# The two Mamba scans of a four-block kernel: from a scan by state over 128 channels to scan tiles of 32 channels x 4 states

## What is computed

```
xz = x @ Win.T ; u, z = split(xz)                        # 256 channels each
u  = silu(causal_conv4(u) + convb)
dtr, B, C = split(u @ Wx.T, [8, 24])                      # 16 states
dt = softplus(dtr @ Wdt.T + bdt) ; A = -exp(Alog)         # [256, 16]
h[t] = exp(dt[t] * A) * h[t-1] + (dt[t] * u[t]) * B[t]    # 256 x 16 states
y[t] = sum over n of h[t, :, n] * C[t, n] + u[t] * D
out  = (y * silu(z)) @ Wout.T
```

## Time and profile before

| | us |
|---|---|
| median of 3 runs (1869.71 to 1870.5) | 1870.18 |
| the profiled execution | 1869.97 |
| its span in the trace | 1868.0 |
| forward pass: preparation / scan / output | 82.55 / 241.65 / 13.4 |
| backward pass: preparation / scan | 76.85 / 242.05 |

### The profile page before, as it was taken

The page is one execution under the profiler, slowest core; times in us unless marked ns, Lnnn a source line. Parts: engine busy times, 40 slices in busy tenths (PEclk is TensorE's granted clock), DMA queues, the critical chain, the costliest instruction groups (busy, mean ns, idle before and its releaser), DMA issues. The chain is left out here.

```text
span 1868.0 us, 19573 instructions
## 1 busy us (share of the span) xinstructions
PE 1461.9 (78%) x6816; PEld 551.5 (30%) x6816; DVE 1388.6 (74%) x1944; ACT 948.8 (51%) x1147; POOL 375.1 (20%) x349
## 2 busy tenths in 40 slices
PE   0441499999999999999665777766577777699998
PEld 0220022222222222222221222232122223467776
DVE  8933899999999999994467999964799997311111
ACT  2220077777777777778445555523555453244332
POOL 1201000000000000000203666640266665000000
PEclk9765599999999999999876999997599999699999
DMA  0021010001000000000000000000000000000000
GB/s 28 0 76 70 25 53 1 1 31 44 2 1 38 38 2 1 2 1 1 11 0 0 1 0 1 1 5 6 0 1 1 0 1 3 22 14 23 11 23 22
DMA packets 19444, 26.14 MB, mean 14 GB/s; under 512 B 4078, under 2 KB 13958, under 8 KB 19358
## 3 DMA queue, kind: packets, MB, share of 16 engines
q1 hardware_dynamic: 19358, 25.06, 3.9%
HBM read 20.56 MB, written 4.19 MB: 13 GB/s over the span
## 5 line engine op out<-in xcount | busy, mean ns | idle before, releaser
L655 DVE TENSOR_REDUCE at_mpart<-psum 128x1 f32<-128x512 f32 x1024 | 656.8, 686 | 49.5 <-PE psum L720 39.7
L634 ACT ACTIVATE at_probs<-psum 128x1024 f32<-128x1024 f32 x512 | 496.2, 1021 | 273.3 <-PE psum L745 273.1
L1070 ACT ACTIVATE psum<-m_dt,m_aneg 128x512 f32<-128x512 f32 x256 | 176.9, 692 | 224.2 <-DVE m_h L1098 224.2
L716 PE MATMUL psum<-at_ks,at_qs 64*128 64x512 bf16 x512 | 207.7, 406 | 86.1 <-DMA at_km<-k_parts 51.8
L758 PE MATMUL psum<-at_probs,at_vg 128*32 128x512 f32 x2048 | 273.6, 606 | 0.4 <-ACT at_probs L634 0.4
L745 PE MATMUL psum<-at_qs,at_ks 75*128 75x512 bf16 x1024 | 269.1, 384 | 1.3 <-ACT at_probs L634 0.2
L720 PE MATMUL psum<-at_km,at_qm 64*128 64x512 bf16 x512 | 207.7, 406 | 0.0
L1112 POOL TENSOR_TENSOR msb_hc<-m_h,msb_crow 128x512 f32<-128x512 f32 x128 | 159.7, 1269 | 155.8 <-DVE m_h L1098 155.8
L1112 POOL TENSOR_TENSOR msf_hc<-m_h,msf_crow 128x512 f32<-128x512 f32 x128 | 159.7, 1269 | 145.0 <-DVE m_h L1098 143.8
L1141 PE MATMUL psum<-msb_hc,ident 128*128 128x512 f32 x256 | 142.9, 644 | 55.0 <-POOL msb_hc L1112 48.9
L1141 PE MATMUL psum<-msf_hc,ident 128*128 128x512 f32 x256 | 142.2, 640 | 55.5 <-POOL msf_hc L1112 49.2
(11 more groups left out here) (245 smaller groups left out, 1344.9 us busy)
## 6 DMA issues: line engine op xcount, KB each, us to landing
at_qs<-q_parts SPq DMA_DIRECT2D x48, 96.0 KB
at_ks<-k_parts SPq DMA_DIRECT2D x48, 96.0 KB
xe_w<-in_w SPq DMA_DIRECT2D x16, 256.0 KB
q_parts<-ap_parts SPq DMA_DIRECT2D x1, 1536.0 KB, 5.3
k_parts<-ap_parts SPq DMA_DIRECT2D x1, 1536.0 KB, 5.3
at_qm<-q_parts SPq DMA_DIRECT2D x16, 96.0 KB
at_km<-k_parts SPq DMA_DIRECT2D x16, 96.0 KB
l_x<-in_x SPq DMA_DIRECT2D x4, 256.0 KB
```

The lines of the kernel that those rows point to most:

```text
L634: act.activation(probs[:, u % 2, p, :], s_pair[p], ACT.Exp, scale=float(HD) ** -0.5).then_inc(probs_ready, 1)
L655: dve.reduce_max(mpart[:, s % 2, 2 * jp + b, i, kc:kc + 1], ring[x % 3], AX.X).then_inc(ring_free, 1)
L716: pe.matmul(ring[x % 3], S.qs[0:HALF, buf, q], S.ks[0:HALF, buf, k], start=True, stop=True)\
L1070: act.activation(decay[b], S.dt[:, b, cols(k)], ACT.Exp, scale=S.aneg[:, NS * b + n:NS * b + n + 1]).then_inc(decay_ready, 1)
```

## The change

**Preparation.** The convolution moves into the weights: VectorE multiplies the u half of Win by the four taps, PE adds four products over shifted inputs in PSUM, and ACT applies silu with the bias straight from PSUM, by chunks of 512, through a ring of 8 PSUM banks. B and C are no longer split; B, C, dt and dt*u are stored to DRAM by chunks. GpSimd makes dt*u.

**Scan.** A scan tile has 32 channels x 4 states on its 128 partitions. `k` runs over 4 chunks x 2 blocks x 4 groups of states x 4 groups of channels, 128 steps; 16 steps are a block. dt and dt*u of a block (copied to the four groups of partitions) and B and C of a chunk (spread over 32 partitions each) come from DRAM by DMAs of 32 partitions. In a step GpSimd makes dt*u*B, ACT the decay, VectorE scans into PSUM and then weighs the tile of the step before by C. ACT keeps the last column. Every four steps PE adds four tiles by four products of 32 output columns each.

The diff, cut to its core:

```diff
@@ -872,10 +870,18 @@
...
 BC = 2 * NS
...
+GC = 32
+SP4 = P // GC
+NQ = NS // SP4
+NJ = P // GC
+NTILE = (DI // GC) * NQ
...
 def mamba_prep_stage(nc, S, dr, d):
...
@@ -886,154 +892,163 @@
...
+        soft, dt, dtu = sb("soft", [P, NB, T]), sb("dt", [P, NB, T]), sb("dtu", [P, NB, T])
...
+        UZ = 2 * NB * NCH
+        ORDER = [("x", 0)]
+        for c in range(NCH):
+            if c + 1 < NCH:
+                ORDER.append(("x", c + 1))
+            ORDER += [("d", c, b) for b in range(NB)]
+        USE = {key: UZ + n for n, key in enumerate(ORDER)}
...
         @block.sync
...
+            for k in range(KC):
+                sp.dma_start(taps[:, k, :], dr["taps"][d, k:k + 1, :].to_broadcast([P, DI])).then_inc(taps_in, 16)
...
+            for c in range(NCH):
+                sp.wait_ge(ring_free, USE["x", c] + 1)
+                sp.dma_start(S.bc_dram[:, cols(c)], bcx[0:BC, cols(c)]).then_inc(bc_stored, 16)
+            for c in range(NCH):
+                sp.wait_ge(dt_ready, c + 1)
+                sp.dma_start(S.dt_dram.rearrange("(b p) t -> p b t", p=P)[:, :, cols(c)],
+                             dt[:, :, cols(c)]).then_inc(dt_stored, 16)
+                sp.wait_ge(dtu_ready, c + 1)
+                sp.dma_start(S.dtu_dram.rearrange("(b p) t -> p b t", p=P)[:, :, cols(c)],
+                             dtu[:, :, cols(c)]).then_inc(dtu_stored, 16)
...
         @block.gpsimd
...
+            for c in range(NCH):
+                pool.wait_ge(dt_ready, c + 1)
+                pool.tensor_tensor(dtu[:, :, cols(c)], dt[:, :, cols(c)], S.u[:, :, cols(c)],
+                                   ALU.mult).then_inc(dtu_ready, 1)
...
         @block.scalar
...
+            for c in range(NCH):
+                for b in range(NB):
+                    act.wait_ge(ring_full, use + 1)
+                    act.activation(S.u[:, b, cols(c)], ring[use % R], ACT.Silu, bias=V(f"{name}_convb{b}"))\
+                        .then_inc(ring_free, 1)
+                    use += 1
+                for b in range(NB):
+                    act.wait_ge(ring_full, use + 1)
+                    act.activation(S.zs[:, b, cols(c)], ring[use % R], ACT.Silu).then_inc(ring_free, 1)
+                    use += 1
...
+            for key in ORDER:
+                act.wait_ge(ring_full, use + 1)
+                if key[0] == "x":
+                    act.activation(bcx[:, cols(key[1])], ring[use % R][0:BC + DR, :], ACT.Copy).then_inc(ring_free, 1)
+                else:
...
+                    act.activation(soft[:, b, cols(c)], ring[use % R], ACT.Abs, bias=V(f"{name}_bdt{b}"))
+                    act.activation(dt[:, b, cols(c)], ring[use % R], ACT.Relu, bias=V(f"{name}_bdt{b}"))\
+                        .then_inc(ring_free, 1)
+                    if b == NB - 1:
+                        act.wait_ge(ring_free, use + 1)
+                        act.activation(soft[:, :, cols(c)], soft[:, :, cols(c)], ACT.Exp, scale=-1.0).then_inc(exp_ready, 1)
+                use += 1
+            for c in range(NCH):
+                act.wait_ge(exp_ready, c + 1)
+                act.activation(soft[:, :, cols(c)], soft[:, :, cols(c)], ACT.Ln, bias=1.0).then_inc(ln_ready, 1)
...
         @block.vector
...
+            for c in range(NCH):
+                dve.tensor_scalar(xm[:, KC - 1 + c * CH:KC - 1 + (c + 1) * CH], S.xh[:, d, cols(c)], V("norm_g"), V("norm_b"),
+                                  ALU.mult, ALU.add).then_inc(xm_ready, 1)
+                if c == 0:
+                    dve.wait_ge(taps_in, 16 * KC)
...
+                    dve.tensor_tensor(taps[:, :, :], taps[:, :, :],
+                                      w_in_sb[:, 0:DI].unsqueeze(1).to_broadcast([P, KC, DI]), ALU.mult).then_inc(taps_ready, 1)
             for b in range(NB):
...
+            for s in range(SP4):
...
+            for c in range(NCH):
+                dve.wait_ge(ring_free, USE["d", c, NB - 1] + 1)
+                dve.wait_ge(ln_ready, c + 1)
+                dve.tensor_tensor(dt[:, :, cols(c)], dt[:, :, cols(c)], soft[:, :, cols(c)], ALU.add).then_inc(dt_ready, 1)
...
         @block.tensor
...
+            pe.wait_ge(taps_ready, 1)
...
+            for c in range(NCH):
+                pe.wait_ge(xm_ready, c + 1)
                 for b in range(NB):
...
+                    for k in range(KC):
+                        mm = pe.matmul(ring[use % R], taps[:, k, P * b:P * (b + 1)], xm[:, c * CH + k:(c + 1) * CH + k],
+                                       start=(k == 0), stop=(k == KC - 1))
+                    mm.then_inc(ring_full, 1)
+                    use += 1
                 for b in range(NB):
...
+                    pe.matmul(ring[use % R], w_in_sb[:, DI + P * b:DI + P * (b + 1)],
+                              xm[:, KC - 1 + c * CH:KC - 1 + (c + 1) * CH], start=True, stop=True).then_inc(ring_full, 1)
+                    use += 1
+            for key in ORDER:
...
+                if key[0] == "x":
+                    c = key[1]
+                    pe.wait_ge(ring_free, 2 * NB * c + NB)
+                    for b in range(NB):
+                        mm = pe.matmul(ring[use % R][0:BC + DR, :], w_x[:, b, :], S.u[:, b, cols(c)],
+                                       start=(b == 0), stop=(b == NB - 1))
+                else:
...
+                    pe.wait_ge(ring_free, USE["x", c] + 1)
+                    mm = pe.matmul(ring[use % R], w_dt[BC:BC + DR, P * b:P * (b + 1)], bcx[BC:BC + DR, cols(c)],
+                                   start=True, stop=True)
+                mm.then_inc(ring_full, 1)
+                use += 1
...
 def mamba_scan_stage(nc, S, dr, d):
...
@@ -1047,98 +1062,146 @@
...
+        PB = NQ * NJ
+        PC = NB * PB
+        NK = NCH * PC
+        ND, NI, NH2 = 3, 4, 3
...
+        def at(k):
+            c, rest = divmod(k, PC)
+            b, rest = divmod(rest, PB)
...
+        dts, dus = sb("dts", [P, 2, NJ, CH]), sb("dus", [P, 2, NJ, CH])
+        bs, cs = sb("bs", [P, 2, NQ, CH]), sb("cs", [P, 2, NQ, CH])
+        inject = sb("inject", [P, NI, CH])
+        last = sb("last", [P, PC])
+        hc = sb("hc", [P, 2, NJ, CH])
+        decay, hv, y_bank = S.banks[0:3], S.banks[3:6], S.banks[6:8]
...
+        bc_in = [sem("bc_in0"), sem("bc_in1")]
...
+        @block.sync
+        def _(sp):
+            for i in range(NCH * NB):
...
+                if i >= 2:
+                    sp.wait_ge(decay_ready, PB * (i - 1))
+                    sp.wait_ge(injected, PB * (i - 1))
+                rows = slice(P * b, P * (b + 1))
+                for s in range(SP4):
+                    part = slice(GC * s, GC * (s + 1))
+                    sp.dma_start(dts[part, i % 2, :, :], S.dt_dram[rows, cols(c)].rearrange("(j p) t -> p j t", p=GC))\
+                        .then_inc(dt_in[i % 2], 16)
+                    sp.dma_start(dus[part, i % 2, :, :], S.dtu_dram[rows, cols(c)].rearrange("(j p) t -> p j t", p=GC))\
+                        .then_inc(du_in[i % 2], 16)
+                if b == 0:
+                    if c >= 2:
+                        sp.wait_ge(injected, PC * (c - 1))
+                        sp.wait_ge(weighed, PC * (c - 1))
+                    for s in range(SP4):
+                        part = slice(GC * s, GC * (s + 1))
+                        for t, off in ((bs, 0), (cs, NS)):
+                            sp.dma_start(t[part, c % 2, :, :],
+                                         S.bc_dram[off:off + NS, cols(c)].rearrange("(o q s) t -> s o q t", o=1, s=SP4)[s]
+                                         .to_broadcast([GC, NQ, CH])).then_inc(bc_in[c % 2], 16)
...
         @block.scalar
...
+            def keep(k):
+                if k >= 0 and k + PC < NK:
+                    act.wait_ge(weighed, k + 1)
+                    act.activation(last[:, k % PC:k % PC + 1], hv[k % NH2][:, CH - 1:CH], ACT.Copy)\
+                        .then_inc(kept, 1)
...
             for k in range(NK):
...
+                if k % PB == 0:
+                    act.wait_ge(dt_in[i % 2], 16 * SP4 * (i // 2 + 1))
+                if k >= ND:
+                    act.wait_ge(scanned, k - ND + 1)
+                n = NQ * (NJ * b + j) + q
+                act.activation(decay[k % ND], dts[:, i % 2, j, :], ACT.Exp, scale=S.aneg[:, n:n + 1]).then_inc(decay_ready, 1)
+                keep(k - 2)
+            keep(NK - 2)
+            keep(NK - 1)
...
         @block.vector
...
+            def weigh(k):
...
+                dve.wait_ge(scanned, k + 1)
+                dve.wait_ge(bc_in[c % 2], 16 * 2 * SP4 * (c // 2 + 1))
+                if r >= 2:
+                    dve.wait_ge(summed, r - 1)
+                dve.tensor_tensor(hc[:, r % 2, j, :], hv[k % NH2], cs[:, c % 2, q, :], ALU.mult).then_inc(weighed, 1)
...
+            def gate(i):
...
+                dve.wait_ge(summed, NQ * (i + 1))
+                gated = S.zs[:, b, cols(c)]
+                dve.tensor_tensor(gated, gated, y_bank[i % 2], ALU.mult).then_inc(y_free, 1)
...
```

(81 more changed lines are left out.)

235 lines of the change are left out of this document (57 added, 178 removed).

## The result

The kernel before took 1869.95 us (median of 4 runs, 1869.63 to 1870.5), the changed kernel 1905.01 us (4 runs, 1902.71 to 1908.4): 1.0191 times as long, 95% interval 1.0174 to 1.0209. The forecast was 1901 (1876 to 1930), slower.

What follows compares the result with a forecast made beforehand. VectorE was taken to bound the scan, a chain of whole-row steps the preparation. Preparations +8.9 for both, plus 2 x (18.1 start - 7.0 stream and tail), made +31.1 us on 1869.97: 1901, range 1876 to 1930.

Steps and rivals of the forecast that it cites:

- Stream and tail, -7.0 us a pass: Scan stage, first scan to next stage: steps of 1.78 us, stream 228.9 plus tail 3.8, against 235.0 plus 4.7 before.
- The cover: Scan step: GpSimd's injection, ACT's decay and column copy, and PE's sums stay hidden beside VectorE's 1.78 us step.
- The price of a scan into PSUM: Scan step: writing the scan to PSUM changes a step by -0.10 to +0.12 us, taken as 0.
- longer step: Rival, scan step: PSUM writing or the weighing, copy and decay loop adds 0.12 us a step, 1932 us; chance 0.08.
- cheaper step: Rival, scan step: PSUM writing saves up to 0.16 us a step, 1860 us; chance 0.14 together with a much shorter start.
- The start, +18.1 us a pass: Scan stage start: 4.19 MB load uncovered at 255 GB/s, 16.4 us; first scan 20.1 us in, against 2.0 before.
- slower loads: Rival, scan start: DMAs onto 32 partitions run at 150 to 230 GB/s; at 190, +5.7 us a pass, 1912; chance 0.24.
- Loads that stay hidden above 148 GB/s: Scan stage after its start: double-buffered loads, up to 4.19 MB per 28.4 us block, stay hidden above 148 GB/s.
- The preparation, 84.2: Each preparation stage lasts 84.2 us, +7.3 against the backward 76.85 and +1.6 against the forward 82.55.
- PE's products over 8 rows ran at the slow rate: Preparation: B, C and dt products might run at 0.86 us a pass as before, putting ACT's end at 65 us.
- The 20.6 us for PE: Preparation: PE's time for B, C and dt at the slow rate, where ACT needs 17.4 us.
- The gain of the convolution on PE (four VectorE steps less) is given back: Preparation: 24 more f32 products, 20.6 us, and a tail of small steps, GpSimd's product and the store cancel the gain.

Runs made afterwards that it cites:

- early loads: Against the changed kernel, only the first inputs of each scan are loaded earlier, during the preparation; 1878.3 us, 1.0054 of the kernel before.
- wide loads: Against the changed kernel, partition is 4 x channel + state, so each scan load reaches all 128 partitions; 1904.6 us, 1.0181 of the kernel before.

## Why the prediction was right, and where it was off

The time, the sign and the mechanism came as forecast. That the sum is right to 4 us is partly luck: the start was too low and the preparations too high, and stage by stage the change cost 39.8 us where 31.1 were forecast; in the profiled execution 6 us of scatter in untouched stages hid most of that difference.

- *Stream and tail, -7.0 us a pass.* Right: 1.78 us a step, stream 230.0 against 228.9, tail 3.5 against 3.8; that makes -6.2, and the early loads show the same alone. The cover held: from the second scan on VectorE waited for nothing but the last sum, so GpSimd, the column copy and PE delayed nothing.
- *The price of a scan into PSUM, between -0.10 and +0.12, taken as 0.* Shown to be 0 (1.78 and 1.775 us a step; the scan itself 1.18 and 1.19). The rivals "longer step" and "cheaper step" fall.
- *The start, +18.1 us a pass.* This is the mis-sized term: +22.1 in the forward pass of the profiled execution. The step that failed is "I take 255 GB/s, the nearest row": the earlier trace rows is of loads onto all 128 partitions, these go onto 32 and ran at 213. 4.19 MB at 213 are 19.7 us, and 2.3 of latency make 22.0 of the 22.8. The row was no measure of wide loads either, and not "in rows of that length": it averages two unlike microseconds (349 and 162 GB/s, below), in the second of which the 16-byte rows of a bias came in, and 695 of its 814 packets are shorter than 2 KB. The rival "slower loads" (190 GB/s, +5.7 us a pass) had the cause, which the wide loads show for dt and dt*u; its size was 4.0. By the figure of the Trainium skill ("SBUF — State Buffer", Door 1) the first scan would have come 22.1 + 3.7 = 25.8 us into the stage, an estimate; it came at 24.1, and the forecast had 20.1.

```profile
1631.00:1632.00 1.00, 0.00 (x0) 0.00 (x0) 0.00 (x0) 0.00 (x0) 0.00 (x0) 0.50 1.06 349
1632.00:1633.00 1.00, 0.00 (x0) 0.00 (x0) 0.00 (x0) 0.00 (x0) 0.00 (x0) 0.50 1.19 162
```

- *Loads that stay hidden above 148 GB/s.* Right: VectorE has no gap at block or chunk starts.
- *The preparation, 84.2.* 82.9 and 83.1. The start and PE's end were right (u and z end 43.5 us in against 42.4). The carry-over of "PE's products over 8 rows ran at the slow rate" failed: four passes take 1.98 us here, 0.5 each, because PE comes to them from the products for u and z at the upper clock level (granted clock 1.00 from 961 to 971); ACT then set the pace and its last exp ended at 62.8 instead of 65. The 20.6 us for PE was also a miscount: it fits 24 passes, and B, C and dt are 32, 27.5 us at 0.86; it did no harm, since they did not run so. GpSimd's four products took 12.1 us, not 11.1: 3.0 each beside VectorE's adds.
- *"The gain of the convolution on PE (four VectorE steps less) is given back."* More than given back: undoing it wins 10 to 14 us a preparation. The forecast compared with the old preparation as a whole and did not see this loss by itself.
- *The sum.* +31.1 forecast; the profiled span grew by 33.8: scans 10.1 more than forecast, preparations 2.3 less, output stages 0.9 more, untouched stages 6 less. Against the medians the change cost 35.1.
